# Second attention of a two-layer block: first pass on all 128 rows, stack matmuls queued one item ahead, GpSimd's bias addition moved

## What is computed

```python
q = (x @ Wqa @ Wqb).reshape(b, s, H, D)              # H = 16 heads, D = 8
kv = (x @ Wkva @ Wkvb).reshape(b, s, KVH, D, 2)      # KVH = 4 groups
k, v = (kv[..., 0], kv[..., 1])
q = _rope(q)
k = _rope(k)
k = jnp.repeat(k, g, axis=2)
v = jnp.repeat(v, g, axis=2)
scores = jnp.einsum('bqhd,bkhd->bhqk', q, k) * scale
scores = jnp.where(causal[None, None], -jnp.inf, scores)
w = jax.nn.softmax(scores, axis=-1)
out = jnp.einsum('bhqk,bkhd->bqhd', w, v).reshape(b, s, E)
return out @ Wout + bout
```

## Time and profile before

| | us |
|---|---|
| median of 3 runs | 1278.17 |
| lowest and highest of them | 1269.31, 1282.07 |
| the profiled execution | 1282.22 |
| its span, first to last instruction | 1280.4 |
| PE busy | 1148.3 |
| DVE busy | 928.0 |
| ACT busy | 756.3 |
| POOL busy | 174.5 |
| mean granted clock of PE | 0.917 of 2.4 GHz |

### The profile page before, as it was taken

How to read it: one execution, slowest core, us unless ns; L and a number is a source line. 1 busy time by engine, 2 the same in 40 slices (tenths; PEclk the granted TensorE clock), 3 DMA queues, 4 the chain that set the end, 5 groups by cost and what they waited for, 6 DMA issues and landing times.

```text
span 1280.4 us, 17685 instructions
## 1 busy us (share of the span) xinstructions
PE 1148.3 (90%) x6034; PEld 620.2 (48%) x6047; DVE 928.0 (72%) x1803; ACT 756.3 (59%) x1112; POOL 174.5 (14%) x142
## 2 busy tenths in 40 slices
PE   3888668599999788999999999999997799999998
PEld 2333344477777423333233322322223688888886
DVE  4699986356555746688896869898932788888885
ACT  1635435477888322456565756566776666666664
POOL 0000000488899300000000000000000000000000
PEclk9898777899999865899997979998999799999999
DMA  5000011999985300000000000000000211111001
GB/s 166 1 0 1 0 46 30 220 228 217 200 192 128 132 1 1 2 2 2 2 1 2 2 1 2 1 1 1 2 1 1 93 58 58 58 58 57 0 2 33
DMA packets 37467, 64.01 MB, mean 50 GB/s; under 512 B 14346, under 2 KB 27914, under 8 KB 32010
## 3 DMA queue, kind: packets, MB, share of 16 engines
q1 hardware_dynamic: 37394, 63.04, 19.9%
HBM read 59.68 MB, written 3.21 MB: 49 GB/s over the span
## 4 chain that ended last, share of the span: by engine, by line
PE 62%; DVE 25%; ACT 5%; issue 4%; DMA 2%; POOL 1%; SPq 1%; DVEq 0%; POOLq 0%; ACTq 0%
PE ps L1069 10%; PE ps L862 9%; PE ps L864 9%; PE ps L863 9%; PE ps L998 7%; DVE arena_b L1815 6%; PE ps L1047 4%; PE ps L959 4%; DVE arena_b L1566 3%; PE ps L1011 2%; DMA arena_a<-root_weights 2%; PE ps L1054 1%; DVE arena_b L1747 1%; ACT arena_b L1379 1%; POOL parts L690 1%
## 5 line engine op out<-in xcount | busy, mean ns | idle before, releaser
L1379 ACT ACTIVATE arena_b<-ps 128x1024 f32<-128x1024 f32 (+3 forms) x320 | 275.1, 895 | 156.3 <-PE ps L1047 134.3
L862 PE MATMUL ps<-parts 128*128 128x512 f32 x640 | 254.3, 397 | 21.8 <-POOL parts L690 19.4
L863 PE MATMUL ps<-parts 128*128 128x512 f32 x640 | 250.5, 391 | 0.0
L864 PE MATMUL ps<-parts 128*128 128x512 f32 x640 | 250.3, 391 | 0.0
L1815 DVE TENSOR_REDUCE arena_b<-ps 128x1 f32<-128x512 f32 x384 | 237.6, 683 | 15.4 <-PE ps L998 14.0
L998 PE MATMUL ps<-arena_a 48*128 48x128 bf16 (+3 forms) x832 | 188.4, 324 | 10.8 <-DVE arena_b L1815 3.2
L690 POOL TENSOR_TENSOR parts<-arena_b,parts 128x512 fp32r<-128x512 f32 x128 | 166.4, 1310 | 70.5 <-ACT parts L1316 66.2
L1069 PE MATMUL ps<-arena_b 128*32 128x512 f32 (+3 forms) x1280 | 160.4, 575 | 0.0
L1047 PE MATMUL ps<-arena_a 50*128 50x512 bf16 (+3 forms) x832 | 152.6, 320 | 4.9 <-issue 2.6
L998 PEld LDWEIGHTS ps<-arena_a 48*128 48x128 bf16 x832 | 60.6, 97 | 186.1 <-DVE arena_b L1815 115.4
L1747 DVE SCALAR_TENSOR_TENSOR arena_b<-ps,arena_a 128x512 f32<-128x512 f32 x128 | 86.8, 688 | 87.7 <-PE ps L864 64.5
(11 more groups left out here) (265 smaller groups left out, 1172.5 us busy)
## 6 DMA issues: line engine op xcount, KB each, us to landing
arena_a<-root_weights SPq DMA_DIRECT2D x62, 512.0 KB, 7.8
arena_b<-expert_weights SPq DMA_DIRECT2D x7, 1024.0 KB, 6.7
wslot<-in_L_ffn_up_w SPq DMA_DIRECT2D x8, 256.0 KB, 7.0
wslot<-in_L_ffn_down_w SPq DMA_DIRECT2D x8, 256.0 KB, 9.1
root_weights<-arena_b SPq DMA_DIRECT2D x4, 512.0 KB, 7.0
wslot<-in_L_ffn_w_gate SPq DMA_DIRECT2D x8, 256.0 KB, 3.0
wslot<-in_L_ffn_w_up SPq DMA_DIRECT2D x8, 256.0 KB, 3.7
wslot<-in_L_ffn_w_down SPq DMA_DIRECT2D x8, 256.0 KB, 4.2
```

The costliest lines, as they stand in the source:

```text
L862: mm(bank, w(0), x(0), start=start, stop=False)
L863: mm(bank, w(0), x(1), start=False, stop=False)
L864: return mm(bank, w(1), x(0), start=False, stop=stop)
L1379: a(probs[:, s % 2, 2 * pair:2 * pair + 2, off:CW], ps[:, 2 + 2 * pair:4 + 2 * pair, off:CW], ACT.Exp, scale=scale).then_inc(p2_exp, 1)
```

## The change

Seven edits:

- `kst` gets a second copy (`take([2, G1, T], BF16)`). The key stack's result is written by two ACT instructions of 64 partitions each, rows 0 to 63 into copy 0, rows 64 to 127 into copy 1, in place of one of 128. GpSimd writes zeros into the other half of each copy once, after layer 0's experts, and PE's first slot waits for both.
- The first pass multiplies all 128 rows of `qst` with copy `i % 2`; the zeros take out the other strip. The second pass keeps its 50 rows.
- Only the 3 stacks of item 0 are made ahead (`PRE = NEEDED[0]`); the 3 of item n + 1 are spread among the first-pass blocks of item n, for every n. 45 stacks are slots now, 36 were.
- `SLOTS[0]` ends with item 0's maxima: 20 slots, 3 of them stacks. The lists beside steps 0 to 3 hold 28 slots (20 before), those beside steps 4 to 47 hold 229 (224), those beside steps 48 to 143 hold 380 (374).
- The rule for how many slots a step gets aims at the end of an item's maxima.
- GpSimd's bias addition waits for the fourth item's maxima (`nm_ready` at 4) in place of the third normalised chunk.
- Items are named by a list `ITEMS`, whose order is the same. A memset on DVE is written for an order in which a later item is of an earlier chunk; with this order it makes no instruction.

```diff
+    for c, g in ITEMS:
+        for x in [(a, g, 0) for a in range(c + 1)] + [(c, g, 1), (c, g, 2)]:
+            if x not in stacks:
+                stacks.append(x)
+        needed.append(len(stacks))
...
-            if c < NC - 1 and (len(blocks) - 1 - k) < HPG - 1:
-                scores.append(("stack", -1, c + 1, n % G1, k + HPG - 1 - len(blocks)))
             if k == 0 and n > 0:
                 scores.append(("maxima", n - 1))
+            scores += [("stack", -1) + x for x in ahead[k * len(ahead) // len(blocks):(k + 1) * len(ahead) // len(blocks)]]
     scores.append(("maxima", NITEM - 1))
-    slots = [scores[:end[1]]]
-    done = end[1]
+    end = {n: scores.index(("maxima", n)) + 1 for n in range(NITEM)}
+    done = end[0]
+    slots = [scores[:done]]
...
-        for n in range(2, NITEM):
+        for n in range(1, NITEM):
             if first[n] - 3 >= k:
-                want = min(end[n] + HPG + 1, len(scores)) - done
+                want = end[n] - done
...
-        kst = take([G1, T], BF16)
+        kst = take([2, G1, T], BF16)
...
-        PRE = 3 * G1
+        PRE = NEEDED[0]
...
-            pool.wait_ge(ln_xn, 3 * NC)
+            pool.wait_ge(moe_down, N_IT0 * MU)
+            pool.wait_ge(moe_prod, N_IT0 * MU)
+            g.memset(kst[STRIP:P, 0].rearrange("p g t -> p (g t)").bitcast(F32), 0.0).then_inc(kzero, 1)
+            g.memset(kst[0:STRIP, 1].rearrange("p g t -> p (g t)").bitcast(F32), 0.0).then_inc(kzero, 1)
+
+            pool.wait_ge(nm_ready, G1)
             pool.wait_ge(wo1_ready, 1)
             g.tensor_tensor(xt[:, :, :], xt[:, :, :], bo1[:, :].unsqueeze(1).broadcast_to([P, NT, D]), ALU.add)\
                 .then_inc(bias_ready, 1)
...
-                    pe.wait_ge(stack_ready, 3 * (n + 1))
-                    r = slice(STRIP * (i % 2), STRIP * (i % 2) + KROWS)
+                    pe.wait_ge(stack_ready, NEEDED[n])
+                    if m == 0:
+                        pe.wait_ge(kzero, 2)
...
-                        return mm(b[:, at_:at_ + kw], qst[r, g, tq // TPC, i // 2, tq % TPC * P:(tq % TPC + 1) * P], kst[r, g, k0:k0 + kw],
+                        return mm(b[:, at_:at_ + kw], qst[:, g, tq // TPC, i // 2, tq % TPC * P:(tq % TPC + 1) * P], kst[:, i % 2, g, k0:k0 + kw],
...
-                    return mm(ps[:, 2 + 2 * pair + i, lo:hi], kst[r, g, j * P:(j + 1) * P],
+                    return mm(ps[:, 2 + 2 * pair + i, lo:hi], kst[r, i, g, j * P:(j + 1) * P],
...
-                    a(kst[:, g, chunk(c)], ps[:, bank, :], ACT.Identity, bias=onerow[:, :]).then_inc(stack_ready, 1)
+                    for half in range(2):
+                        r = slice(half * STRIP, half * STRIP + STRIP)
+                        last = a(kst[r, half, g, chunk(c)], ps[r, bank, :], ACT.Identity, bias=onerow[r, :])
+                        if half == 0:
+                            step(last)
+                    last.then_inc(stack_ready, 1)
```

More of the change, by code:

```diff
@@ L47 @@
 STRIP = 64
-NITEM = NC * G1
+ITEMS = tuple((c, g) for c in range(NC) for g in range(G1))
+NITEM = len(ITEMS)
+LAST_OF = {c: n for n, (c, g) in enumerate(ITEMS)}
 E1, F1 = 8, 512
@@ L61, in attention_schedule @@
 def attention_schedule():
-    steps = [(n, j) for n in range(NITEM) for j in range(TPC * (n // G1 + 1))]
+    steps = [(n, j) for n, (c, _) in enumerate(ITEMS) for j in range(TPC * (c + 1))]
     first = {}
@@ L71, in attention_schedule @@
         first.setdefault(n, k)
+    stacks, needed = [], []
+    for c, g in ITEMS:
[3 more added lines that the diff above has]
+        needed.append(len(stacks))
     scores = []
-    for n in range(NITEM):
-        c = n // G1
+    for n, (c, _) in enumerate(ITEMS):
         blocks = [("scores", t, u) for t in range(TPC * c, TPC * c + TPC) for u in range(c)]
         blocks += [("diag", 0, 0), ("below3", 0, 0), ("below12", 0, 0)]
+        ahead = stacks[needed[n]:needed[n + 1]] if n + 1 < NITEM else []
         for k, (what, t, u) in enumerate(blocks):
             scores += [(what, n, t, u, i) for i in range(HPG)]
-            if c < NC - 1 and (len(blocks) - 1 - k) < HPG - 1:
-                scores.append(("stack", -1, c + 1, n % G1, k + HPG - 1 - len(blocks)))
             if k == 0 and n > 0:
                 scores.append(("maxima", n - 1))
+            scores += [("stack", -1) + x for x in ahead[k * len(ahead) // len(blocks):(k + 1) * len(ahead) // len(blocks)]]
     scores.append(("maxima", NITEM - 1))
-    end = {n: max(k for k, x in enumerate(scores) if x[1] == n and x[0] != "maxima") + 1 for n in range(NITEM)}
-    slots = [scores[:end[1]]]
-    done = end[1]
+    end = {n: scores.index(("maxima", n)) + 1 for n in range(NITEM)}
+    done = end[0]
+    slots = [scores[:done]]
     late = {}
-    for n in range(NITEM):
-        s = first[n] + TPC * (n // G1 + 1)
+    for n, (c, _) in enumerate(ITEMS):
+        s = first[n] + TPC * (c + 1)
         late.setdefault(s + 1, []).append(("out", n))
-        if n % G1 == G1 - 1:
-            late.setdefault(s + 2, []).append(("turned", n // G1))
-            late.setdefault(s + 3, []).append(("product", n // G1))
+        if n == LAST_OF[c]:
+            late.setdefault(s + 2, []).append(("turned", c))
+            late.setdefault(s + 3, []).append(("product", c))
     for k in range(len(steps)):
         rate = 0
-        for n in range(2, NITEM):
+        for n in range(1, NITEM):
             if first[n] - 3 >= k:
-                want = min(end[n] + HPG + 1, len(scores)) - done
+                want = end[n] - done
                 rate = max(rate, -(-want // (first[n] - 2 - k)))
@@ L105, in attention_schedule @@
     tail = [x for k in sorted(late) for x in late[k]]
-    return steps, slots, tail
+    return steps, slots, tail, stacks, needed
 def adaln_two_layers(nc, A, out):
@@ L375, in adaln_two_layers @@
         vzero = sem("vzero")
+        kzero = sem("kzero")
         wt_tr = sem("wt_tr")
@@ L422, in adaln_two_layers @@
         out_ready = sem("out_ready")
-        STEPS, SLOTS, LAST_SLOTS = attention_schedule()
+        STEPS, SLOTS, LAST_SLOTS, STACKS, NEEDED = attention_schedule()
         NFIRST = len(SLOTS[0])
-        PRE = 3 * G1
-        STACKS = [(c, g, kind) for c in range(NC) for g in range(G1) for kind in range(3)]
+        PRE = NEEDED[0]
         def slot_bank(m):
@@ L441, in slot_before @@
             return ORDER[same[-1]] if same else None
+        assert [x[2:] for x in ORDER if x[0] == "stack"] == STACKS[PRE:]
         NITEM0 = min(k for k, x in enumerate(SLOTS[0]) if x[1] == 1 or x[0] == "maxima")
@@ L1024, in slot @@
                     c = what[1]
-                    pe.wait_ge(slot_read, READ["out", c * G1 + G1 - 1])
+                    pe.wait_ge(slot_read, READ["out", LAST_OF[c]])
                     for k, t in enumerate(tiles(c)):
@@ L1062, in values @@
                 n, j = STEPS[s]
-                c, g = n // G1, n % G1
+                c, g = ITEMS[n]
                 off = max(0, j - TPC * c) * P
@@ L1812, in slot @@
                     _, n, t, u, i = what
+                    c = ITEMS[n][0]
+                    if n >= 2 and c < ITEMS[n - 2][0] and (what[0] == "scores" and (t, u) == (TPC * c, 0)
+                                                           or what[0] == "diag" and c == 0) and i == 0:
+                        chain(v.memset(mx[:, n % 2, :, :, 4 + c:7], -BIG))
                     m8 = mx[:, n % 2, 2 * (i % 2) + i // 2]
```

12 lines of the change are left out of this document (6 added, 6 removed).

## The result

The kernel became slower: 1295.92 us median of 4 runs (1295.11 to 1296.72), against 1274.10 for the kernel before in the same comparison (4 runs, 1269.31 to 1282.07), ratio 1.0175 [1.013, 1.022]. 1248 with a range up to 1267 had been forecast. The profiled execution took 1296.72 us (span 1294.9), 14.5 more than the one of before.

What follows compares the result with a forecast made beforehand. The prediction took DVE as nearest to full at full clock, and PE as the bound where the clock is low inside items. Its terms summed to -33.9 us from the profiled 1282.2, giving 1248, range 1235 to 1267.

Steps and rivals of the forecast that it cites:

- C: Item 0's first pass and the work behind it, ahead of step 0: 128-row blocks bring the clock up, -3 us.
- E: Falls of the clock inside items 8 to 13: full-height first-pass matmuls hold the clock up, -20.6 us together.
- F: Key stack's copy in two ACT instructions of 64 partitions, delaying the bank and next exponential: +3 us (0 to 10).
- G: First-pass strips no longer overlap: 20.7 us more for PE, mostly covered by waits for DVE, +4 us (0 to 20).
- A: Stacks made ahead of the first item: nine fewer of twelve, at 1.36 us each, -12.2 us.
- B: Between the values and step 0: ten slots fewer, the maxima's transfer now waited for, 16.4 us become 7, -9.4 us.
- D: More slots in the steps: steps 0 to 3 -2.7 us, steps 4 to 47 +3.1, steps 48 to 143 +3.9.
- the last rival: PE becomes the bound: first-pass weight loads no longer hidden behind the other strip, 1297 us, chance 0.07.
- The second rival: Only busy time counts for the clock, not rows: no gain in items 8 to 13, 1286 us, chance 0.13.
- The first: Rival: clock comes back only in part, low stretches staying in steps 0 to 3 or some items; 1263 us, chance 0.18.
- H: GpSimd's two memsets beside the normalisation and its moved bias addition: 0 us (-3 to +4).

Runs made afterwards that it cites:

- e6: Kernel before, with both passes on 128 rows ahead of step 0 and in the first two and last four steps of each item, strips between: 1251.43 us, 0.9827.
- e2: Kernel before with the 128-row first pass, the zeros and the two key copies, in the old order: 1292.80 us, 1.0176.
- e3: Kernel after with the second pass (scores) on all 128 rows too: 1279.20 us, 1.0054.
- e5: Kernel after with the two score pairs of a step next to each other, no first-pass blocks between: 1276.82 us, 1.0031.
- e10: e6 with a third key-stack copy instruction of 64 partitions, writing the same values again: 1270.07 us, 0.9991.
- e1: Kernel after with its first pass again in 48-row strips; zeros, both key copies and new order stay: 1294.66 us, 1.0189.
- e4: Kernel before with only the new order of stacks and the late bias addition; 48-row strips, one key copy, no zeros: 1281.03 us, 1.0078.
- e8: e4 with only chunk 0's stacks queued one item ahead, later chunks' stacks in their old places: 1273.62 us, 0.9946.
- e12: e6 with 128 rows only ahead of step 0 and in items 0 to 3, strips from item 4 on: 1269.83 us, 0.9999.
- e7: Kernel after (new order) with e6's rows, full only ahead of step 0 and at the items' edges: 1258.49 us, 0.9871.
- e11: e6 with GpSimd's bias addition moved behind the fourth item's maxima: 1252.54 us, 0.9869.
- e9: e8's order, with the bias behind the fourth item, and e6's rows: 1250.03 us, 0.9842.

## Why the prediction was wrong

The three steps from the kernel before over e6 and e2 to after take the change apart, by the profiled executions. Items 1 to 14 together: before 417.6 us, e6 399.2, e2 436.0, after 451.5.

| step | where | forecast | measured |
|---|---|---|---|
| full rows (C) | first exponential, before to e2 | -3 | -5.5 |
| the clock held, two copies (E, F) | items 1-14, before to e6 | -17.6 | -18.4 |
| full rows everywhere, strips' overlap lost (G) | items 1-14, e6 to e2 | +4 | +36.8 |
| stacks and slots moved ahead of step 0 (A, B) | first exponential, e2 to after | -21.6 | -13.6 |
| more slots in the steps (D) | items 1-14, e2 to after | +7.0 | +15.5 |
| item 0 (D) | before to after | -2.7 | -1.2 (rows -5.6, order +4.4) |

The line between the second row and the third isn't sharp, since e6 has full rows in both passes at the edges. Where the clock is full both times, G shows by itself: from before to e2, items 4 to 7 grow by 7.3 us and item 9 by 4.0.

**The step that failed is G**: "Where DVE is the bound, PE waits for it (115.4 us, rows 3), so most is covered: +4". Two readings in it were wrong.

First, the cover. The 115.4 us are idle time of the weight loads' own row. A load may go ahead while the matmul before it still runs (e3's load at 860.69 above), so its wait for DVE can hold time in which PE was at work. PE's own slack stood in the earlier trace rows: 99.12 of 102.90 us busy in items 4 to 7, 3.8 us free. The argument against the last rival, that this time held modelled ends, was too weak: once PE's work grew, DVE's wait before its 512-column reductions went from 3.2 to 14.7 us.

Second, the price. Only the lost overlap of first-pass pairs was charged. The rows compared were matmuls of 128 rows next to each other, and for these the load is hidden, as e3 shows too. But the change puts 128-row matmuls between 50-row ones, a case that no row of before was taken for. The kernel held it all along, where mask matmuls of 128 rows stand between 48-row ones. PE's timeline of before at full clock, each line 512 columns in all:

```profile
472.41 0.39 PE L998 MATMUL ps<-arena_a 48*128 48x128 bf16 x4
472.73 0.39 PE L1011 MATMUL ps<-maskqk,identb 128*128 128x512 bf16 x1
473.06 0.39 PE L998 MATMUL ps<-arena_a 48*128 48x128 bf16 x4
```

They start 0.32 and 0.33 us apart.

The last rival named the mechanism, a load laid bare and PE the bound, and its 1297 us is 1 us from the result; but it priced the load at every matmul of the first pass. That it came within 1 us is luck. The runs show the load at the changes of height: e5, with two changes fewer per step, saves 19 us, e3 with almost none 17. Counted in the traces of items 1 to 14, PE's matmul has another height or width of weights than the one before it 653 times in before, 1003 after, 978 in e2, 768 in e5, 388 in e6 and 318 in e3. From after to e5 that is 235 changes fewer and 19.3 us less in these items, 0.08 us each.

The rule of the Trainium skill (TensorE: Matmul & The Clock Gate, section "The mechanism") that a weight load overlaps a running matmul only when the row groups differ is contradicted where both have all rows (0.227 us apart in e3), and agrees with the trace where a full-height and a strip's matmul, which share rows, alternate. Taking the first for a refutation of the whole rule was the mistake.

**E was right, and C in the old order.** The clock goes by the rows that have work, and not by PE's busy time alone. Every kernel with full rows throughout or at the edges has no half clock in items 1 to 14, but for 3.4 us in e10; every one with strips at the edges falls (before 48 us, e1 32, e4 15, e8 68, e12 34). e12 against e6 shows that the rows at the edges make the difference, and e6's gaps at full clock (4.38 of 5 us busy) that busy time alone does not. The second rival is refuted. The first is too in the main: the wait before step 0 did lower the clock, for 6 us of item 0, but the falls in items 1 to 14 that its 1263 needed didn't come. What the Trainium skill's section "What's actually happening" names, how busy PE is, does show in e10, where gaps in the stage ahead delay the clock's rise; e12 and e6 show that it isn't all. E also started from a profiled execution at the slow end (1282.2, where 54 more runs in three groups have medians of 1270 to 1272), so some 10 us of the -33.9 were not there against the median.

**A and B.** The stacks ahead fell from 16.3 to 5.1 us (-11.2, forecast -12.2). The last stretch is 7.0 us, as worked out (the terms given there add up to 7.2), with 2.9 us of it PE's wait for the maxima's transfer. The stretch between, where C had -3, grew from 18.5 to 19.3, since 15.0 us of it were at half clock, where it had been 11.6; with the stacks' later start (0.7) the first exponential came 19.1 us earlier in place of 24.6. Item 0 took 21.3 us, 4.4 more than in e2.

**D was mis-sized.** A stack was charged 0.64 us like any slot. It holds its bank until ACT has copied it, and where it was looked at PE waits and DVE idles behind it (e4). In e7 against e6, clock held in both, items 1 to 14 cost 18.0 us in place of 7, 15.9 of them in items 4 to 14. Thus the order (D with A and B) gains 13.5 us before step 0 and loses it all later: +7 in e7 against e6, +9 in e4 against before. What is taken from ahead of step 0 comes back beside the steps.

**F** was +3. Each copy of 64 partitions takes 0.68 us, as taken. The second one costs 0.27 us per three stacks in the stage ahead. Where the clock holds, nothing of it is seen in the steps (items 4 to 7 take 102.4 us in e6, 102.9 before), but no run has full rows and one copy, so it isn't priced there. Where it doesn't hold, copies and zeros cost 13.6 us together (e4 to e1), more than F's upper bound of 10. A third copy costs 18.6 us (e10).

**H** was 0, and e11 bears out the bias. The memsets took 3.5 us each and not 3.6; they end at 432 us. Two small DVE instructions beside them take 1.5 us each in place of 0.17. That isn't why the stacks start 0.7 us later: with the memsets and the old order e2 starts them at 454.42 us, as before (454.45), and e4, which has no memsets, at 455.29. Single executions move the start by as much (e11).

## What to carry to other kernels

Before a matmul is given another height, look at its neighbours on PE: beside matmuls of the same height and width the load stayed hidden here, at each change it lay bare for about 0.1 us, and only PE's own slack (span less busy), not the wait in the row of its weight loads, can cover it. Rows with zeros can hold the clock, but they are wanted only where it falls, here a few steps at the edges of each item: that turned a loss of 1.8% (e2) into a gain of 1.7% (e6). Where DVE is the bound, a slot that another engine reads, here a stack, costs DVE's idle time (1.61 us in the one looked at) and not the 0.64 us of a mean slot.

## What the runs showed of the hardware that had not been expected

- The clock depends on the height of the matmuls too. With the same instructions in the same order, 128 rows in the steps at the edges of items give no half clock in items 1 to 14, and 48 to 50 rows give 34 us of it (e6, e12).
- Where the clock falls, runs of one kernel can be far apart (before 14.7 us over 23 runs, e8 21.0 over 10); those of after, e5, e6 and e9, whose clock holds in items 1 to 14, lie within 1.1 to 2.0 us. It is no rule: e2, e7 and e11 hold it too and have 6 to 8 us.
- A third copy of 0.68 us on ACT delays the first exponential by 8.5 us (e10 against e11) over four groups of stacks: 0.3 is a later start and some 2.9 the copies themselves (4 x 0.72); over the rest the clock is lower, as it comes up later when PE has gaps.
- A weight load of 0.1 us is hidden between two matmuls of 128 rows that follow each other (0.227 us apart), and bare between one of 128 and one of 50 rows (0.31 to 0.32), and between weights of 128 columns and of 32 (0.32).
